# Two PSUM banks for exponentials taken one bank at a time, four for maxima taken two banks at a time, and the loops of layer 1 written out

## The chip, the cores and the metric

The kernel runs on one NeuronCore of a Trainium2 chip. The metric is the device time of one execution in microseconds (us). The kernel before was timed in three runs: median 14171.25 us, from 14164.81 to 14183.32.

The engines that matter are TensorE (PE in the profile, with its weight loads as PEld), VectorE (DVE), ScalarE (ACT) and, less, GpSimd (POOL) and the DMA queues of SyncE (SP) and POOL. Each works through its own list of instructions in order; semaphores tie them together.

## The reference

Two layers on an image batch x of 8 x 56 x 56 x 128. Layer 0 is a spectral mixing layer and is not touched by the change. Layer 1 is attention with 8 heads of 16 channels over the 3136 positions of each image, a residual and a layer norm:

```python
q = proj(wq, bq)
k = proj(wk, bk)
v = proj(wv, bv)
scores = jnp.einsum('bhqd,bhkd->bhqk', q, k) / jnp.sqrt(jnp.float32(d_k))
scores = scores + _spatial_bias_matrix(spatial_bias, H, W)[None, None]
attn = jax.nn.softmax(scores, axis=-1)
ctx = jnp.einsum('bhqk,bhkd->bhqd', attn, v)
...
resid = out + x_seq
...
out = (resid - mu) * jax.lax.rsqrt(var + LN_EPS) * ln_gamma + ln_beta
```

The bias of a score depends only on the distance of the two positions, rows plus columns, so it is added by a matmul over a small window table.

## The kernel before

Layer 0 takes the first 1.5 ms, some tables 0.3 ms more, and layer 1 the rest, from about 1.8 ms to the end.

**Tiling of layer 1.** Images `B` = 8, groups of four heads `NG` = 2, chunks `NC` = 7 of `CH` = 448 queries (8 rows of 56). So there are 112 chunks, numbered n. Within a chunk the 3136 keys are worked through in `EX` = 56 steps k: t = k // 2 is a tile of 112 keys and k % 2 a pair of the four heads. The softmax needs the largest score of each query first, so a chunk has two jobs that run side by side: the exponentials of chunk n, and the maxima of chunk n + 1 (`MX` = 112 tiles i of 112 queries x 448 keys).

**TensorE's order within a step k** is written out by hand (the function `step` at L1021 to L1053):

- `scores(g, k, between)` makes the scores of two heads e = 0, 1: two matmuls of keys by queries (L914, side by side in one PSUM bank) and two that add the bias (L918). Between e = 0 and e = 1 it calls `between`, that is `next_max`.
- `next_max` issues, if one is due, the two matmuls of one tile of maxima (`max_scores`, L947). `ahead(k, g, c)` says how many tiles are due by step k: all 112 in the first 49 steps, 16 in 7 steps, so that a step has 2 or 3 of them. An even step calls `next_max` before its scores (step 0 twice), then between the heads, after them, and last; an odd step has no call before its scores. In chunk 6 of a group the maxima begin at step 4 (`K_LATE`), in chunk 0 of an image at step 6 (`K_NEXT`).
- In odd steps from 3 on, `weigh` multiplies the exponentials of steps k - 3 and k - 2 with the values (L930, eight fp32 matmuls, in four column groups side by side). The last two steps of a chunk are weighed in step 0 of the next.
- Side work in the bank `MB`: the sums of the chunk before at step 3 (L982), its output product at step 10 for the second group (L989), the row maxima at step 52 (`turn_rows`, L956), and in chunk 5 of a group the projections of the next group, one of 42 pieces a step from step 12 (L967, L971, L975).

**ScalarE** takes one exponential a step (L1116) over two PSUM banks, 120 partitions x 896, into one of four buffers `p`; at step 2 it copies the context of the chunk before (L1094), at step 52 two row maxima (L1089), and in chunk 5 the projections (L1080). **VectorE** takes a maximum for every tile i (`find_max`, L1194), 120 x 448 each, and does the small work: copies for the next chunk (L1178, L1188, L1189), reciprocals at steps 5 to 8 (L1214), the layer norm of the second group from step 11, the split of the projections (L1161). **GpSimd** converts projections and issues loads and stores, **SyncE** issues the keys of the maxima (`key_win`).

**PSUM's eight banks** are shared out at L716: four for scores awaiting the exponential (`SB`), two for each step, so TensorE may fill step k while ScalarE reads step k - 1; one for the context (`CB`); two for the maxima (`AB`); one for side work (`MB`).

**The waits.** `exp_ready` is raised once a step, and `exp_done` once a step (it starts at 2). Before the scores of step k TensorE waits until the exponential of step k - 2 is done (L1034); before the maxima of tile i it waits until tile i - 2 has been reduced (L944).

**Loops.** `images` runs seven images in a hardware loop and writes the eighth out; `chunks` writes out chunks 0, 5 and 6 of a group and runs chunks 1 to 4 in a hardware loop, on TensorE, ScalarE and VectorE. In a loop a wait's threshold is worked out in a register. SyncE and GpSimd have loops of their own over chunks.

## Time and profile before

| | us |
|---|---|
| median of 3 runs | 14171.25 (14164.81 to 14183.32) |
| the profiled execution: its own time | 14178.28 |
| its span, first to last instruction | 14176.7 |
| mean granted TensorE clock | 0.949 of full |
| PE busy | 13118.8 (93%) |
| DVE busy | 10007.6 (71%) |
| ACT busy | 6425.9 (45%) |
| POOL busy | 891.7 (6%) |

The span is the time from the first to the last instruction on the core; 1.6 us of the profiled execution's time lie outside it. Busy is the time in which an engine had at least one instruction in work; matmuls overlap, so for PE it says little about how densely the starts follow each other. For that one reads the starts in the timeline.

### The profile page before, as it was taken

What the parts mean: (1) busy time and instruction counts of PE and PEld (TensorE: products, weight loads), DVE (VectorE), ACT (ScalarE), POOL (GpSimd) and SP (SyncE); (2) the same over time, 40 slices, a digit from 0 to 9 for tenths busy, and PEclk for the clock granted to TensorE, in tenths of its full rate; (3) what the DMA queues carried; (4) which work ended last, traced back from release to release, by engine and by line L of the source; (5) the groups of instructions that cost most, each with busy time, mean ns of one, the idle gap of its engine ahead of it and who ended that gap; (6) DMA issues with size and microseconds to landing.
All of it is one profiled execution on the core that took longest, in us unless ns stands there. A gap on an engine that the chain in (4) does not pass through costs nothing.

```text
span 14176.7 us, 304054 instructions
## 1 busy us (share of the span) xinstructions
PE 13118.8 (93%) x110635; PEld 5455.4 (38%) x110635; DVE 10007.6 (71%) x17426; ACT 6425.9 (45%) x7576; POOL 891.7 (6%) x1062
## 2 busy tenths in 40 slices
PE   8888479999999999999999999999999999999999
PEld 4444123333333333333333333333333333333333
DVE  3555167777777777777777777777777777777776
ACT  1111025554555545554555455545555455545555
POOL 0222110001000000000000100000000000010000
PEclk8888569999999999999999999999999999999999
DMA  3443122222222222222222222222222222222121
GB/s 65 88 88 80 43 41 35 39 41 40 36 37 42 40 38 37 41 40 39 36 40 38 42 35 37 42 40 39 38 39 40 39 40 37 39 42 40 36 38 30
DMA packets 317569, 607.72 MB, mean 43 GB/s; under 512 B 63894, under 2 KB 248750, under 8 KB 315054
## 3 DMA queue, kind: packets, MB, share of 16 engines
q1 hardware_dynamic: 294618, 535.94, 20.8%
q0 software_dynamic: 21504, 51.47, 1.3%
q8 instruction: 1033, 16.92, 0.5%
q14 instruction: 414, 3.39, 0.1%
HBM read 328.18 MB, written 53.47 MB: 27 GB/s over the span
## 4 chain that ended last, share of the span: by engine, by line
PE 71%; DVE 9%; issue 5%; ACT 2%; DVEq 0%; SPq 0%; DMA 0%; ACTq 0%; POOL 0%; POOLq 0%
PE l_ps L947 18%; PE l_ps L930 17%; PE l_ps L914 15%; PE l_ps L918 15%; DVE partial L1194 6%; PE l_ps L971 3%; PE l_ps L989 1%; PE l_ps L982 1%; ACT q_max L1089 1%; PE l_ps L975 1%; ACT p L1116 1%; DVE recip L1214 1%; DVE win_exp L1189 0%; DVE qs L1161 0%; DVE ks L1161 0%
## 5 line engine op out<-in xcount | busy, mean ns | idle before, releaser
L1194 DVE TENSOR_REDUCE partial<-l_ps 120x1 f32<-120x448 f32 x12544 | 7356.3, 621 | 2001.3 <-PE l_ps L947 1988.3
L1116 ACT ACTIVATE p<-l_ps 120x896 f32<-120x896 f32 x6272 | 5722.9, 917 | 5605.3 <-PE l_ps L918 5536.5
L947 PE MATMUL l_ps<-key_win,q_pick 128*56 128x448 f16 (+1 forms) x25088 | 4482.2, 365 | 407.4 <-DVE partial L1194 259.9
L914 PE MATMUL l_ps<-q_exp,ks 65*56 65x448 f16 (+1 forms) x25088 | 4543.4, 361 | 40.5 <-DVE win_exp L1189 27.7
L918 PE MATMUL l_ps<-win_exp,fold 112*56 112x448 f16 x25088 | 4513.8, 359 | 0.0
L930 PE MATMUL l_ps<-p,v 120*32 120x448 f32 x25088 | 3052.5, 559 | 2.1 <-ACT p L1116 2.1
L947 PEld LDWEIGHTS l_ps<-key_win,q_pick 128*64 128x64 f16 (+1 forms) x25088 | 1331.5, 108 | 3913.8 <-DVE partial L1194 3171.9
L914 PEld LDWEIGHTS l_ps<-q_exp,ks 65*64 65x64 f16 (+1 forms) x25088 | 1403.1, 110 | 1189.2 <-issue 282.6
L918 PEld LDWEIGHTS l_ps<-win_exp,fold 112*56 112x56 f16 x25088 | 1381.3, 109 | 924.3 <-issue 42.4
L930 PEld LDWEIGHTS l_ps<-p,v 120*32 120x32 f32 x25088 | 499.6, 109 | 1052.4 <-issue 1021.1
L866 POOL CAST half<-full 128x448 f16<-128x448 f32 x448 | 270.4, 604 | 5959.3 <-ACT full L1080 5959.3
L392 PE MATMUL l_ps<-G,Y 112*120 112x448 f32 x1024 | 425.7, 581 | 140.0 <-DVE Y L564 140.0
L1205 DVE CAST q_max<-l_ps 1x448 f16<-1x448 f32 x224 | 138.3, 617 | 521.8 <-PE l_ps L956 518.4
L881 POOL DMA_DIRECT2D out<-res x112 | 72.1, 648 | 5635.0 <-DVE res L1295 5069.4
L1214 DVE RECIPROCAL recip<-l_ps 128x112 f32<-128x112 f32 x448 | 376.2, 845 | 69.7 <-PE l_ps L982 69.7
L573 DVE TENSOR_TENSOR x<-l_ps,x 56x448 f32<-56x448 f32 x256 | 159.0, 621 | 289.5 <-PE l_ps L392 285.5
L1161 DVE SCALAR_TENSOR_TENSOR qs<-half,flags_sb,full 64x448 f16<-64x448 f16 x448 | 304.1, 679 | 66.1 <-POOL half L866 34.7
L392 PEld LDWEIGHTS l_ps<-G,Y 112*120 112x120 f32 x1024 | 201.7, 199 | 360.7 <-issue 328.7
L1161 DVE SCALAR_TENSOR_TENSOR ks<-half,flags_sb,full 64x448 f16<-64x448 f16 x448 | 306.1, 683 | 25.7 <-ACT q_max L1089 8.9
L479 ACT COPY xt<-l_ps 128x448 f32<-128x448 f32 x32 | 17.0, 532 | 584.4 <-PE l_ps L416 584.4
L971 PE MATMUL l_ps<-xT,wk 128*128 128x448 f32 x448 | 243.5, 627 | 38.3 <-DVEq L1207 27.6
L1080 ACT ACTIVATE full<-l_ps,bq 128x448 f32<-128x448 f32 x224 | 142.3, 635 | 285.3 <-PE l_ps L971 274.1
(135 smaller groups left out, 5520.5 us busy)
## 6 DMA issues: line engine op xcount, KB each, us to landing
key_win<-ks SPq DMA_DIRECT2D x1792, 112.0 KB, 2.8
key_win<-by_query_scratch SPq DMA_DIRECT2D x224, 868.0 KB, 5.9
x<-in_x SPq DMA_DIRECT2D x16, 1568.0 KB
xc<-y_scratch POOLq DMA_DIRECT2D x224, 112.0 KB, 2.7
h_scratch<-x SPq DMA_DIRECT2D x8, 1568.0 KB
w_scratch<-x SPq DMA_DIRECT2D x8, 1568.0 KB
mh<-h_scratch SPq DMA_DIRECT2D x64, 196.0 KB
mw<-w_scratch SPq DMA_DIRECT2D x64, 196.0 KB
```

Of the source, the lines that this page charges most:

```text
L392: last = nc.tensor.matmul(ps[0:GP + W, IB + i % 2, 0:HALF], w["Y"][:, k, (i // 2) * 2 * GP:(i // 2) * 2 * GP + GP + W], w["G"][r][:, k, (i ...
L573: nc.vector.tensor_tensor(dst, ps[GP * odd:GP * odd + W, IB + i % 2, 0:HALF].rearrange("p (t s) -> p t s", s=S), dst, ALU.add).then_inc(ad ...
L866: nc.gpsimd.tensor_copy(half[m][:], full[m][:]).then_inc(proj_half, 1)
L914: nc.tensor.matmul(ps[r * GP:r * GP + m, bank, 0:CH], ks[g][:, j, k0:k0 + m], q_exp[:, j, :], start=True, stop=True)
L918: last = nc.tensor.matmul(ps[r * GP:r * GP + W, bank, 0:CH], fold16[:], win_exp[:, s0:s0 + CH], start=False, stop=True, skip_group_check=True)
L930: last = nc.tensor.matmul(ps[32 * j:32 * j + 32, CB, 0:CH], v[g][:, v0:v0 + 32], p[k % 4][:, e, :], start=t == 0, stop=t == NT - 1, skip_g ...
L947: last = nc.tensor.matmul(ps[r * GP:r * GP + wide, AB + i % 2, 0:CH], q_pick[:, j, q0:q0 + wide], rows(key_win[place][:])[:, s0:s0 + QC, 0 ...
L971: nc.tensor.matmul(ps[:, MB, 0:CH], (wk4 if i % 2 == 0 else wq4)[:, h:h + 2, :].rearrange("c h k -> c (h k)"), rows(xT[:])[:, :, 0:W], sta ...
L1116: nc.scalar.activation(p[k % 4][:], ps[0:GP + W, bank:bank + 2, 0:CH], ACT.Exp).then_inc(exp_done, 1)
L1161: last = nc.vector.scalar_tensor_tensor(dst, rows(half[pn % 3][part, :], W), w["flags"][part, 0:1] if is_k else w["flags"][part, 1:2], row ...
L1194: nc.vector.tensor_reduce(partial[:, tile, kc:kc + 1], ps[0:GP + W, AB + i % 2, 0:CH], AX.X, ALU.max).then_inc(max_done, 1)
L1214: nc.vector.reciprocal(recip[:, cut], ps[:, MB, cut]).then_inc(recip_done, 1)
```

## The change

PSUM is shared out anew: two banks for scores awaiting the exponential (`SB` = 0), four for maxima (`AB` = 2), then the context (`CB` = 6) and side work (`MB` = 7). Each head e of a step has one bank. TensorE raises `exp_ready` after each head, ScalarE takes the exponential of one bank (120 x 448) and raises `exp_done` after each, and before the scores of head e in step k TensorE waits for the exponential of the same head in step k - 1. The maxima are reduced in pairs of tiles: one VectorE instruction over two banks (120 x 2 x 448) for each odd i, and TensorE waits before every even i from 4 on until the pair before the last has been reduced. The loops over images and over chunks 1 to 4 are written out for every engine that uses these two helpers: TensorE, ScalarE and VectorE wholly; GpSimd's images too, while its inner loops and SyncE's remain.

```diff
--- before.py
+++ after.py
@@ -713,7 +713,7 @@
         res_in, res = sb("res_in", [KT, UT, C]), sb("res", [KT, UT, C])
         stat = sb("stat", [KT, 3, UT])
         ps = ctx.enter_context(nc.psum_tensor("l1_ps", [128, 8, 512], F32))
-        SB, CB, AB, MB = 0, 4, 5, 7
+        SB, AB, CB, MB = 0, 2, 6, 7
 
         loaded, set_up, clear = sem("l1_loaded"), sem("l1_set_up"), sem("clear")
         xc_in, xt_ready = [sem(f"xc{i}_in") for i in range(2)], sem("l1_xt_ready")
@@ -784,15 +784,14 @@
             return FIRST + b * SIDES + place[g, 1, what] + (c - 1) * (place[g, 2, what] - place[g, 1, what])
 
         def images(eng, image):
-            with eng.Fori(0, B - 1) as b:
-                image(b, False)
-            image(B - 1, True)
+            for b in range(B):
+                image(b, b == B - 1)
 
         def chunks(eng, g, last, step):
 
             final = last and g == NG - 1
             step(0, None if g == 0 else NC - 1, True, False)
-            with eng.Fori(1, C_PREP) as c:
+            for c in range(1, C_PREP):
                 step(c, c - 1, True, False)
             step(C_PREP, C_PREP - 1, True, not final)
             step(NC - 1, NC - 2, not final, False)
@@ -904,11 +903,12 @@
 
         @block.tensor
         def _(pe):
-            def scores(g, k, between):
+            def scores(g, n, k, between):
 
                 t, pair = k // 2, k % 2
                 for e in range(2):
-                    j, bank = 2 * pair + e, SB + 2 * pair + e
+                    j, bank = 2 * pair + e, SB + e
+                    pe.wait_ge(exp_done, 2 * (n * EX + k) + e + 1)
                     for r, m in enumerate((GP, W)):
                         k0 = (2 * t + r) * RP
                         nc.tensor.matmul(ps[r * GP:r * GP + m, bank, 0:CH], ks[g][:, j, k0:k0 + m], q_exp[:, j, :],
@@ -917,9 +917,9 @@
                         s0 = (H - 1 - 2 * t - r) * W
                         last = nc.tensor.matmul(ps[r * GP:r * GP + W, bank, 0:CH], fold16[:], win_exp[:, s0:s0 + CH],
                                                 start=False, stop=True, skip_group_check=True)
+                    last.then_inc(exp_ready, 1)
                     if e == 0:
                         between()
-                last.then_inc(exp_ready, 1)
 
             def weigh(g, k):
 
@@ -939,12 +939,12 @@
                     pe.wait_ge(win_in[place], (m + 1) * 16)
                 if kc == 0:
                     pe.wait_ge(keys_in[place], (m * UT * HG // 2 + tile // 2 + 1) * 16)
-                if i >= 2:
-                    pe.wait_ge(max_done, m * MX + i - 1)
+                if i >= 4 and i % 2 == 0:
+                    pe.wait_ge(max_done, m * (MX // 2) + i // 2 - 1)
                 s0 = QC * kc - 2 * u + QC - 2
                 for r, wide in enumerate((GP, W)):
                     q0 = u * KT + r * W
-                    last = nc.tensor.matmul(ps[r * GP:r * GP + wide, AB + i % 2, 0:CH], q_pick[:, j, q0:q0 + wide],
+                    last = nc.tensor.matmul(ps[r * GP:r * GP + wide, AB + i % 4, 0:CH], q_pick[:, j, q0:q0 + wide],
                                             rows(key_win[place][:])[:, s0:s0 + QC, 0:W], start=True, stop=True)
                 last.then_inc(score_ready, 1)
 
@@ -1026,14 +1026,13 @@
                             if k == 0:
                                 next_max()
                                 if before is not None:
-                                    pe.wait_ge(exp_done, 2 + n * EX)
+                                    pe.wait_ge(exp_done, 2 + 2 * n * EX)
                                     for i in (EX - 2, EX - 1):
                                         weigh(g if not (isinstance(c, int) and c == 0) else 1 - g, i)
 
-                            pe.wait_ge(exp_done, 2 + n * EX + k - 1)
                             if k == 0:
                                 pe.wait_ge(staged_exp, HEAD + (n + 1) * 2)
-                            scores(g, k, next_max)
+                            scores(g, n, k, next_max)
                             next_max()
 
                             if k > 1 and k % 2:
@@ -1056,7 +1055,7 @@
                     chunks(pe, g, last, step)
                 n = b * NG * NC + NG * NC - 1
                 for k in range(2):
-                    pe.wait_ge(exp_done, 2 + n * EX + EX - 1 + k)
+                    pe.wait_ge(exp_done, 2 + 2 * (n * EX + EX - 1 + k))
                     weigh(1, EX - 2 + k)
                 spread_sums(n, side(b, last, "end", 0, "sum"))
                 mix(n, side(b, last, "end", 0, "mix"))
@@ -1111,9 +1110,9 @@
                             if k == K_CTX and before is not None:
                                 copy_context(n - 1)
                             act.wait_ge(pv_done, 4 + n * EX + k - 3)
-                            act.wait_ge(exp_ready, HEAD + n * EX + k + 1)
-                            bank = SB + 2 * (k % 2)
-                            nc.scalar.activation(p[k % 4][:], ps[0:GP + W, bank:bank + 2, 0:CH], ACT.Exp).then_inc(exp_done, 1)
+                            for e in range(2):
+                                act.wait_ge(exp_ready, HEAD + 2 * (n * EX + k) + e + 1)
+                                nc.scalar.activation(p[k % 4][:, e, :], ps[0:GP + W, SB + e, 0:CH], ACT.Exp).then_inc(exp_done, 1)
                             if maxima and k == K_ROWS:
                                 copy_rows(side(b, last, g, c, "rows"))
                             if projections and K_PREP <= k < K_PREP + PREP:
@@ -1183,19 +1182,21 @@
                 nc.vector.tensor_copy(q_pick[0:DK], qs[0:DK, :, bass.ds(c * CH, CH)]).then_inc(staged_pick, 1)
 
             def stage_exp(n, c):
-                dve.wait_ge(exp_ready, HEAD + n * EX)
+                dve.wait_ge(exp_ready, HEAD + 2 * n * EX)
                 dve.wait_ge(row_copied, (n + 1) * HG)
                 nc.vector.tensor_copy(q_exp[:], q_max[:]).then_inc(staged_exp, 1)
                 nc.vector.tensor_copy(win_exp[:], w["by_key"][:, bass.ds(c * QC * W, STG_K)]).then_inc(staged_exp, 1)
 
             def find_max(i, base):
-                tile, kc = i // NC, i % NC
+                if i % 2 == 0:
+                    return
+                bank = AB + i % 4 - 1
                 dve.wait_ge(score_ready, AHEAD + base + i + 1)
-                nc.vector.tensor_reduce(partial[:, tile, kc:kc + 1], ps[0:GP + W, AB + i % 2, 0:CH], AX.X,
-                                        ALU.max).then_inc(max_done, 1)
+                nc.vector.tensor_reduce(partial[:].rearrange("p t k -> p (t k)")[:, i - 1:i + 1], ps[0:GP + W, bank:bank + 2, 0:CH],
+                                        AX.X, ALU.max).then_inc(max_done, 1)
 
             def join_max(m):
-                dve.wait_ge(max_done, (m + 1) * MX)
+                dve.wait_ge(max_done, (m + 1) * (MX // 2))
                 nc.vector.tensor_reduce(neg_max[:], partial[:], AX.X, ALU.max, negate=True).then_inc(neg_ready, 1)
 
             def copy_rows(m, n):
@@ -1364,7 +1365,7 @@
                             stage_pick(m + 1, b * 0)
                         elif isinstance(c, int) and c == NC - 1 and maxima:
                             stage_pick(m + 1, b * 0 + 1)
-                        elif not isinstance(c, int) or c == 0:
+                        elif c < C_PREP:
                             stage_pick(m + 1, c + 2)
                     chunks(dve, g, last, step)
                 n = b * NG * NC + NG * NC - 1
```

## Rows read from the trace of the kernel before

**Rows 1.** The page: busy time by engine, one queue's instruction fetches, the chain by engine

```profile
PE 13118.8 (93%) x110635; PEld 5455.4 (38%) x110635; DVE 10007.6 (71%) x17426; ACT 6425.9 (45%) x7576; POOL 891.7 (6%) x1062
...
q8 instruction: 1033, 16.92, 0.5%
...
PE 71%; DVE 9%; issue 5%; ACT 2%; DVEq 0%; SPq 0%; DMA 0%; ACTq 0%; POOL 0%; POOLq 0%
```

**Rows 2.** Windows of image 2's chunks 1, 2, 5: length, busy PE, PEld, DVE, ACT, POOL, clock

```profile
3625.80:3723.90 98.10, 96.14 (x918) 38.36 (x914) 73.31 (x126) 52.56 (x60) 0.00 (x0) 1.00 0.22 39
3723.90:3826.70 102.80, 99.17 (x918) 39.26 (x914) 73.45 (x126) 52.61 (x60) 0.00 (x0) 0.97 0.21 37
...
4029.70:4178.70 149.00, 141.73 (x1056) 56.64 (x1058) 112.64 (x188) 73.75 (x94) 24.71 (x40) 0.96 0.15 28
```

**Rows 3.** Timeline of TensorE in steady steps: start, us, instruction, [idle before <-releaser]

```profile
3741.46 0.35 PE L918 MATMUL l_ps<-win_exp,fold 112*56 112x448 f16 x2
...
3742.23 0.35 PE L914 MATMUL l_ps<-q_exp,ks 65*64 65x448 f16 x2
...
3743.47 0.96 PE L930 MATMUL l_ps<-p,v 120*32 120x448 f32 x8
3744.36 0.57 PE L947 MATMUL l_ps<-key_win,q_pick 128*64 128x448 f16 x4
...
3744.96 0.35 PE L918 MATMUL l_ps<-win_exp,fold 112*56 112x448 f16 x2
3745.47 0.38 PE L947 MATMUL l_ps<-key_win,q_pick 128*64 128x448 f16 x2 [0.15 <-DVE partial L1194]
```

**Rows 4.** Timeline of ScalarE: the exponential after the L918 at 3742.04

```profile
3742.44 1.88 ACT L1116 ACTIVATE p<-l_ps 120x896 f32<-120x896 f32 x2 [1.43 <-PE l_ps L918]
```

**Rows 5.** Timeline in chunk 5 of the last image, where no loop encloses the step

```profile
13988.85 0.35 PE L918 MATMUL l_ps<-win_exp,fold 112*56 112x448 f16 x2
...
13989.31 0.92 ACT L1116 ACTIVATE p<-l_ps 120x896 f32<-120x896 f32 x1 [1.96 <-PE l_ps L918]
```

**Rows 6.** Timeline of steps 53 to 55: exponentials behind the row copies, scores that waited

```profile
3824.07 2.88 ACT L1116 ACTIVATE p<-l_ps 120x896 f32<-120x896 f32 x3
...
3825.04 0.38 PE L914 MATMUL l_ps<-q_exp,ks 65*64 65x448 f16 x2
```

**Rows 7.** Groups by line and shape, ScalarE: busy us, mean ns of one

```profile
L1116 ACT ACTIVATE p<-l_ps 120x896 f32<-120x896 f32 x6272 | 5722.9, 917 | 5605.3 <-PE l_ps L918 5536.5 <-ACT xT L1071 0.2
L1080 ACT ACTIVATE full<-l_ps,bq 128x448 f32<-128x448 f32 x224 | 142.3, 635 | 285.3 <-PE l_ps L971 274.1 <-DVE ks L1161 11.2
...
L470 ACT ACTIVATE mean_t<-l_ps 128x56 f32<-128x56 f32 x16 | 2.6, 205 | 17.4 <-PE l_ps L402 17.4
```

**Rows 8.** The same view, VectorE's reductions

```profile
L1194 DVE TENSOR_REDUCE partial<-l_ps 120x1 f32<-120x448 f32 x12544 | 7356.3, 621 | 2001.3 <-PE l_ps L947 1988.3
...
L1261 DVE TENSOR_REDUCE stat<-res_in 112x4 f32<-112x512 f32 x56 | 38.0, 679 | 0.5
```

**Rows 9.** Timeline from chunk 0 to 1 (no branch), then from 2 to 3 (branch)

```profile
3624.72 0.35 PE L918 MATMUL l_ps<-win_exp,fold 112*56 112x448 f16 x2
...
3627.28 0.38 PE L914 MATMUL l_ps<-q_exp,ks 65*64 65x448 f16 x2
...
3628.32 0.38 PE L947 MATMUL l_ps<-key_win,q_pick 128*64 128x448 f16 x2 [0.48 <-DVE partial L1194]
...
3825.64 0.35 PE L918 MATMUL l_ps<-win_exp,fold 112*56 112x448 f16 x2
...
3829.21 0.95 PE L947 MATMUL l_ps<-key_win,q_pick 128*64 128x448 f16 x4 [2.33 <-issue]
...
3831.74 0.58 PE L914 MATMUL l_ps<-q_exp,ks 65*64 65x448 f16 x2
```

**Rows 10.** Timeline of TensorE in chunk 5 with projections

```profile
4088.15 0.38 PE L947 MATMUL l_ps<-key_win,q_pick 128*64 128x448 f16 x2 [1.38 <-DVE partial L1194]
...
4091.15 1.02 PE L971 MATMUL l_ps<-xT,wq 128*128 128x448 f32 x2
```

## The prediction

> **What bounds the kernel now.** I read the page first: TensorE is busy 93%, VectorE 71%, ScalarE 45%, and the chain that ended last lies to 71% on TensorE and to 9% on VectorE [rows 1]. So TensorE sets the time and the other two cost something only where it waits. How much it waits is in the starts of its matmuls, not in its busy time. Next come windows over single chunks of layer 1: chunk 1 of image 2 takes 98.10 us, chunk 2, which ends in a branch, 102.80, and chunk 5, with projections, 149.00 [rows 2]. In the timeline two steps in a steady stretch are a dense row of slots: from the bias matmuls of the first head to the next step's first scores it is four slots in 0.77, so 0.193 a slot [rows 3]. A chunk has 336 such slots (64.8 us), 28 weighings of 0.89 (3743.47 to 3744.36 [rows 3]) with some 0.09 ahead of each, an estimate (27.4), and the sums (about 1.0, one matmul like that of [rows 10]): 93.2 us with no wait at all. The 98.10 of chunk 1 hold 4.9 us of waits, chunk 2 a further 4.7.
>
> **Edit 1, exponentials of one bank (loses).** Before, the scores of step k needed the exponential of step k - 2. Now head e needs that of head e in step k - 1. Odd steps end with a weighing (0.98 us), which covers this. The crossing from an even to an odd step has no such cover. Its price has four parts.
>
> (a) Matmul to exponential. In a loop the bias matmul at 3742.04 (a slot before the scores at 3742.23 [rows 3]) is followed by its exponential at 3742.44 [rows 4]: 0.40. In the written-out chunk 5 of the last image it is 13988.85 to 13989.31, 0.46 [rows 5]. 
> (b) The exponential of 448. The trace has none. 896 elements take 917 ns and 56 take 205 ns [rows 7], so 0.848 ns an element and 448 take 0.54. Bounds: 0.46, half of 917, and 0.635, an activation of 448 with a bias column [rows 7]. I take 0.54, since line and operands stay the same.
> (c) Back to TensorE. The exponentials from 3824.07 are three; the first ends at 3824.99 and the scores behind it start at 3825.04: 0.05. A matmul that restarts so takes 0.38 in place of 0.35 [rows 3, 6], and the next starts about 0.02 late.
> (d) The distance that is there. With one tile of maxima in between (kind A) 0.77, with a second behind head 1 (B) 0.96, with none (C) 0.58.
>
> The need is 0.46 + 0.54 + 0.05 = 1.05. So A waits 0.28, B 0.09, C 0.47, with the restart 0.30, 0.11, 0.49; for C head 1 is late by 0.03 too, 0.52. Head 1 is else in time: its exponential is due back 1.57 after head 0's bias matmul and its slot comes at 1.65.
> The counts follow from `ahead`: a chunk 1 to 4 has 19 A (steps 0, 2, 4, ... with two tiles), 6 or 7 B (three tiles, and step 52, where the row maxima stand between) and 2 C (50, 54). Chunk 5 has 5 A and 1 C, since side matmuls of up to 1 us fill every step from 12; chunk 6 has 1 A, 23 B, 4 C; the last chunk of all, without maxima, 27 C. Over 112 chunks: 1549 A, 936 B, 288 C. Sum: 465 + 103 + 150 = 718 us. Two places are worse, since ScalarE has something else in front: step 2 (the context copy) by about 0.15, and steps 53 to 55, where the exponentials start only behind the row copies [rows 6] and the scores now need them a step earlier, by about 0.25, half an exponential. That is 0.4 x 112 = 45. In all 763.
> By the Trainium skill (ScalarE: Activation LUTs, its part on what an ACTIVATE costs) one with immediate operands takes 186 ns and 0.833 ns an element, 0.56 for 448. Here 896 elements measured 917 ns where that rule gives 932, so I keep 0.54; by the rule the sum would be 55 us higher.
> What stands behind the new wait on TensorE is everything, since it works in order: the maxima, head 1, the weighing; so VectorE gets its tiles later by as much, and needs them less. The key loads on SyncE's queue wait for maxima long made, as before. The second count of `exp_ready` rides on a matmul that is there.
>
> **Edit 2, maxima by two banks (gains).** The reduction of 448 takes 621 ns and one of 512 takes 679, 0.91 ns an element [rows 8]; two banks take about 1.05 to 1.09 against 2 x 0.58 in a full queue. That saving is off the path. What counts is the slack: TensorE may be two to three tiles further ahead. Now a third tile waits when two follow each other: at 3744.36 two in a row, and the next comes at 3745.47, 0.51 after the bias matmul in place of 0.19 [rows 3]. With the restart that is 0.34, about 6.5 times a chunk: 2.2. At the chunk's start one waits 0.48 [rows 9], at the reciprocals about 0.8 more. Together 3.5 us of the 4.9. The new distance from the second tile of a pair to the first of the pair after next is at least three tile distances, 0.19 + 0.58 + 0.96 = 1.73, and the need 0.40 + 1.09 + 0.05 = 1.54: no wait, unless VectorE has another operation in between. 73 regular chunks (1 to 4, chunk 0 of group 1, the last 5) x 3.5 = 255. Chunk 5: work without waits is 93.2 and the side matmuls, 28 of about 0.96 [rows 10] and 7 x 1.3 for the short ones, 129 in all, against 98 + 36 = 134 at the regular chunk's waits and 149.00 measured; one wait is 1.38 for VectorE [rows 10]. Of these 15 to 20 us VectorE explains a part; I take 6.5, bounds 0 and 13. 15 x 6.5 = 98. Chunk 6 and chunk 0 of group 0 together about 45. Sum 398; bounds 200 (pairs hold up VectorE's other work) and 670 (every wait in the chunks: 4.9 x 97 + 13 x 15).
> In straight code a matmul with two waits (keys and `max_done`) starts 0.04 later; nine of them a chunk, partly given back: 17 us lost.
>
> **Edit 3, loops written out (gains).** From the last bias matmul of chunk 0 to the first scores of chunk 1, with no branch taken, it is 3624.72 to 3627.28, 2.56; with the branch, from chunk 2 to 3, 3825.64 to 3831.74, 6.10, with 2.33 of issue, and the matmuls come at half clock behind it (0.58 for 0.38) [rows 9]. So 3.5 us a branch, 3 branches in each of 16 groups: 167 us. The seven image branches stand behind waits for the layer norm's inputs and give perhaps 3 in all. Register arithmetic in the loops costs nothing now: the 98.10 chunk is in a loop and has it. Fetching: the queue moved 1033 pieces, 16.92 MB [rows 1], which is already the whole executed program, so straight code fetches no more. The prologue's 112 maxima gain about 12.
>
> **Sum.** 763 + 17 - 398 - 167 - 3 - 12 = +200 us on the profiled execution's 14178.28, so 14378. That execution stands 7 us above the median of the runs; against those, 14371.
>
> **Rivals.**
> Forecast: the crossings cost more than slack and branches give, 14371, its own range 14270 to 14480. Chance 0.55.
> No change: head 0's exponential keeps its 0.40. Then each of the 2773 crossings costs 0.06 less, 166 us, and the time is 14205, around the upper edge of no change. Against it speaks every step of the written-out chunks [rows 5]. Chance 0.12.
> Faster: TensorE's waits for the maxima go wholly, 670 in place of 398, also in chunk 5: 200 - 272 = -72, 14099. It decides from 598 us on. For it speaks that VectorE gets 7% of its work back and TensorE twice the slack; against it that chunk 5's waits also come from chains of projections over three engines. Chance 0.14.
> Slower still: VectorE waits for both tiles of a pair with splits and reciprocals queued behind, who free the bank for side work; the gain halves to 200 and chunk 5 grows by 2: 14371 + 198 + 30 = 14600. Chance 0.13.
> The branches' gain doesn't come, since the stall was fetching and straight code stalls as well: 14540. Against it: chunks 4 to 5 to 6 are straight already and go on without a gap. Chance 0.06.
>
> **How the numbers follow.** About 0.2% (28 us) is what a measurement can tell: below 14143 is faster, to 14199 the same. Faster 0.14 and a little of the no-change case, 0.16; same 0.09; slower 0.75. The range runs from 14085 (the faster case in) to 14560; outside are the slower case's 0.13 and the tails of the others.
>
> **What would show it.** L1116 has twice the count at 0.53 to 0.55 each, 0.46 behind the matmul for head 0; idle of L914 before ScalarE's release rises from almost nothing to some 600 us; L1194 halves its count at about 1.09; TensorE's idle before L947 shrinks; no 2.33 of issue between chunks. A regular chunk 1 takes about 102.5 us (98.1 - 3.5 + 7.9). I am wrong if the exponential's start is 0.40 for both heads, if a chunk 5 falls by over 10 us, or if the crossings are hidden by waits that I take to be gone.

## The result, and the profile after

| | before | changed |
|---|---|---|
| median of 6 runs, us | 14170.3 (14164.81 to 14191.61) | 14237.95 (14237.24 to 14240.86) |
| ratio to before, 95% interval | | 1.0045 (1.0032 to 1.0058) |
| span of the profiled execution | 14176.7 | 14239.3 |
| mean granted clock | 0.949 | 0.959 |

The change makes the kernel slower by 0.45%, and the interval lies clear of 1: 68 us by the medians, 63 by the spans of the two profiled executions, which the sums below use. The forecast was 200 us slower. The sign and the mechanism hold, the size is a third of it.

The page of the changed kernel, in order the lines that answer to [rows 1] and two groups that answer to [rows 7, 8]:

```profile
PE 13293.4 (93%) x110635; PEld 5200.0 (37%) x110635; DVE 9484.1 (67%) x11154; ACT 7252.3 (51%) x13848; POOL 889.2 (6%) x1062
...
q8 instruction: 847, 13.88, 0.4%
...
PE 74%; ACT 9%; DVE 2%; issue 2%; ACTq 0%; SPq 0%; DMA 0%; DVEq 0%; POOL 0%; POOLq 0%
...
L1115 ACT ACTIVATE p<-l_ps 120x448 f32<-120x448 f32 x12544 | 6553.4, 543 | 4783.4 <-PE l_ps L918 4704.8
L1195 DVE TENSOR_REDUCE partial<-l_ps 120x2 f32<-120x896 f32 x6272 | 6785.9, 1088 | 2544.9 <-PE l_ps L947 2477.2
```

VectorE lost 523 us of work and ScalarE gained 826, and on the chain that ended last they changed places: it lay to 9% on VectorE and to 2% on ScalarE, and is now 2% and 9%. The exponential of 448 takes 543 ns and the reduction over two banks 1088 ns.

Where TensorE itself stood idle is in the groups of its matmuls (busy us, mean ns, idle before them and its releasers). Before, scores and maxima:

```profile
L914 PE MATMUL l_ps<-q_exp,ks 65*56 65x448 f16 (+1 forms) x25088 | 4543.4, 361 | 40.5 <-DVE win_exp L1189 27.7 <-issue 3.0 <-ACT p L1116 2.8
L947 PE MATMUL l_ps<-key_win,q_pick 128*56 128x448 f16 (+1 forms) x25088 | 4482.2, 365 | 407.4 <-DVE partial L1194 259.9 <-issue 113.5 <-DMA key_win<-ks 6.8
```

The same two groups of the changed kernel:

```profile
L914 PE MATMUL l_ps<-q_exp,ks 65*56 65x448 f16 (+1 forms) x25088 | 4564.2, 363 | 302.8 <-ACT p L1115 113.5 <-DVE win_exp L1188 7.6
L947 PE MATMUL l_ps<-key_win,q_pick 128*64 128x448 f16 (+1 forms) x25088 | 4399.9, 361 | 34.8 <-DVE partial L1195 21.1 <-DMA key_win<-ks 7.0
```

The 113.5 us of issue (the branches) are gone, of the 260 us behind VectorE 21 are left, and 303 us stand before the scores instead of 40. These sums show the direction only: a matmul's modelled end hides most of a short wait, so sizes come from starts, below.

The windows of [rows 2], image 2, chunks 1, 2 and 5 (length, then busy time of PE, PEld, DVE, ACT and POOL, clock, DMA share, GB/s), now:

```profile
3622.30:3724.80 102.50, 99.42 (x918) 36.08 (x914) 68.23 (x69) 60.24 (x115) 0.00 (x0) 1.00 0.20 36
3724.80:3827.30 102.50, 99.41 (x918) 36.09 (x914) 68.23 (x69) 60.15 (x115) 0.00 (x0) 1.00 0.21 37
...
4032.40:4176.30 143.90, 140.72 (x1058) 55.76 (x1058) 108.32 (x132) 79.99 (x150) 24.59 (x40) 0.97 0.16 29
```

Chunk 1 went from 98.10 to the forecast 102.5, chunk 2 lost its branch and is now equal to it, chunk 5 gained 5.1.

The forecast crossing of kind A, in the timeline (start, duration; some rows left out):

```profile
3741.17 0.35 PE L918 MATMUL l_ps<-win_exp,fold 112*56 112x448 f16 x2
...
3741.63 1.06 ACT L1115 ACTIVATE p<-l_ps 120x448 f32<-120x448 f32 x2 [1.48 <-PE l_ps L918]
...
3742.22 0.38 PE L914 MATMUL l_ps<-q_exp,ks 65*64 65x448 f16 x2
```

Bias matmul at 3741.17, its exponential 0.46 later, 0.54 in work, and the next step's scores at 3742.22: 1.05, the need worked out in the prediction. There is no weighing in between, so all of it shows. Over the chunks 1 to 4 of all images the median is 0.459 for head 0 and 0.399 for head 1; for the single exponential of a step it was 0.399 in the loops of the kernel before. From chunk 1 to chunk 2, where nothing branches now:

```profile
3723.32 0.35 PE L918 MATMUL l_ps<-win_exp,fold 112*56 112x448 f16 x2
...
3725.88 0.38 PE L914 MATMUL l_ps<-q_exp,ks 65*64 65x448 f16 x2
```

That is 2.56, as at the boundary without a branch of [rows 9], against 6.10 with one.

### The profile page after: what moved, and what is told of

It is laid out like the page before. It is cut to its first block, busy times and chain, and to the rows that moved or that the text cites. A ratio compares the mean times of both kernels' runs of the same rounds, so it can differ in the third digit from the quotient of the medians.

```text
span 14239.3 us, 268044 instructions
## 1 busy us (share of the span) xinstructions
PE 13293.4 (93%) x110635; PEld 5200.0 (37%) x110635; DVE 9484.1 (67%) x11154; ACT 7252.3 (51%) x13848; POOL 889.2 (6%) x1062
## 3 DMA queue, kind: packets, MB, share of 16 engines
q8 instruction: 847, 13.88, 0.4%
## 4 chain that ended last, share of the span: by engine, by line
PE 74%; ACT 9%; DVE 2%; issue 2%; ACTq 0%; SPq 0%; DMA 0%; DVEq 0%; POOL 0%; POOLq 0%
PE l_ps L930 19%; PE l_ps L914 18%; PE l_ps L947 17%; PE l_ps L918 14%; ACT p L1115 8%; PE l_ps L971 3%; PE l_ps L989 1%; PE l_ps L975 1%; PE l_ps L982 1%; DVE partial L1195 1%; ACT q_max L1088 1%; DVE qs L1160 0%; PE l_ps L967 0%; ACTq L1114 0%; ACT full L1079 0%
## 5 line engine op out<-in xcount | busy, mean ns | idle before, releaser
L1115 ACT ACTIVATE p<-l_ps 120x448 f32<-120x448 f32 x12544 | 6553.4, 543 | 4783.4 <-PE l_ps L918 4704.8
L1195 DVE TENSOR_REDUCE partial<-l_ps 120x2 f32<-120x896 f32 x6272 | 6785.9, 1088 | 2544.9 <-PE l_ps L947 2477.2
L914 PE MATMUL l_ps<-q_exp,ks 65*56 65x448 f16 (+1 forms) x25088 | 4564.2, 363 | 302.8 <-ACT p L1115 113.5
L918 PE MATMUL l_ps<-win_exp,fold 112*56 112x448 f16 x25088 | 4467.9, 356 | 0.0
L947 PE MATMUL l_ps<-key_win,q_pick 128*64 128x448 f16 (+1 forms) x25088 | 4399.9, 361 | 34.8 <-DVE partial L1195 21.1
L914 PEld LDWEIGHTS l_ps<-q_exp,ks 65*56 65x56 f16 (+1 forms) x25088 | 1361.7, 107 | 2904.6 <-ACT p L1115 2443.2
L947 PEld LDWEIGHTS l_ps<-key_win,q_pick 128*56 128x56 f16 (+1 forms) x25088 | 1331.7, 109 | 2852.6 <-issue 1902.8
L918 PEld LDWEIGHTS l_ps<-win_exp,fold 112*56 112x56 f16 x25088 | 1360.5, 108 | 479.7 <-issue 6.4
```

What stands on the lines that cost most here:

```text
L914: nc.tensor.matmul(ps[r * GP:r * GP + m, bank, 0:CH], ks[g][:, j, k0:k0 + m], q_exp[:, j, :], start=True, stop=True)
L918: last = nc.tensor.matmul(ps[r * GP:r * GP + W, bank, 0:CH], fold16[:], win_exp[:, s0:s0 + CH], start=False, stop=True, skip_group_check=True)
L947: last = nc.tensor.matmul(ps[r * GP:r * GP + wide, AB + i % 4, 0:CH], q_pick[:, j, q0:q0 + wide], rows(key_win[place][:])[:, s0:s0 + QC, 0 ...
L1115: nc.scalar.activation(p[k % 4][:, e, :], ps[0:GP + W, SB + e, 0:CH], ACT.Exp).then_inc(exp_done, 1)
L1195: nc.vector.tensor_reduce(partial[:].rearrange("p t k -> p (t k)")[:, i - 1:i + 1], ps[0:GP + W, bank:bank + 2, 0:CH], AX.X, ALU.max).then ...
```

## The experiments

Where a chunk's or a pair of steps' time is given, it is the spacing of the starts of their first score matmuls in the timeline, as a mean over the images. "Group 0" and "group 1" are the head groups. A pair of steps is an even step and the odd one behind it. The experiments fall in three sets, each with its own runs of the kernel before, to which its ratios refer: medians 14186.88, 14189.81 and 14181.06 against the 14170.3 above. A difference of 10 or 20 us between times of different sets is therefore not read from them alone.

### The three parts taken apart

**Loops alone**: the kernel before, with both helpers written out.

```diff
-            with eng.Fori(0, B - 1) as b:
-                image(b, False)
-            image(B - 1, True)
+            for b in range(B):
+                image(b, b == B - 1)
...
-            with eng.Fori(1, C_PREP) as c:
+            for c in range(1, C_PREP):
```

> The kernel before with its loops over images and chunks 1 to 4 written out, banks as before. By the terms of the prediction: 170 us less for the branches, 17 us more for matmuls with two waits, so 14017. Revised theory, after the result: the changed kernel is 137 us below the sum, of which 59 lie in chunk 0 of an image (105.47 us before, 103.58 after, where the sum had +5.5); there VectorE idled 2.33 us for issue between the end of the layer norm and its next copy (3533.43 to 3535.77), which is the image branch on VectorE, so the loops bring 30 to 60 more: 13960 to 13990. Rival: that surplus comes from the four banks for the maxima, not from the loops: 14017 or a little above, and chunk 0 of an image stays near 103 to 105.

Measured: 13976.86 us, ratio 0.9857 (0.984 to 0.9873). The loops' end is worth 197 us by the spans (14176.7 to 13979.9), 210 by the medians of its set. The time lies in the range of the revised theory, but not for its reason: chunk 0 of an image only went from 105.47 to 104.47 us, and 163 of the 197 us are in the chunks 1 to 4 and chunk 0 of group 1.

**Loops and exponentials**: the changed kernel with the maxima as they were, two banks and one tile to an instruction.

```diff
-                if i >= 4 and i % 2 == 0:
-                    pe.wait_ge(max_done, m * (MX // 2) + i // 2 - 1)
+                if i >= 2:
+                    pe.wait_ge(max_done, m * MX + i - 1)
...
-ps[r * GP:r * GP + wide, AB + i % 4, 0:CH]
+ps[r * GP:r * GP + wide, AB + i % 2, 0:CH]
```

> The changed kernel, but with the maxima as before: two banks, one tile to a reduction. Theory additive: loops_only plus the 763 us of the crossings. With 13975 for loops_only that is 14738. Theory overlapping (mine now): a wait for VectorE ahead of the tile between the heads also gives ScalarE time, so about a quarter of the crossings cost nothing: 14520 to 14600. The distance from the changed kernel, 14238, is what the four banks bring: 500 or 280 to 360.

Measured: 14614.11 us, ratio 1.0308 (1.0291 to 1.0325), span 14611.2. So on top of the loops the exponentials cost 631 us (forecast 763), and from here to the changed kernel the maxima's four banks give 372 (forecast 410 with the prologue). Plain addition fails, and of the two theories the overlapping one is nearer, though about a sixth of the crossings' price was covered and not a quarter.

**Image loop alone** written out, chunks 1 to 4 still in their loop.

```diff
-            with eng.Fori(0, B - 1) as b:
-                image(b, False)
-            image(B - 1, True)
+            for b in range(B):
+                image(b, b == B - 1)
```

> The kernel before with only the loop over images written out; chunks 1 to 4 stay in loops. Revised theory (the image branch delays VectorE, and through it the maxima): 30 to 60 us less than before, 14110 to 14140, with no idle for issue ahead of the q_max copy in chunk 0 of an image. By the prediction (image branches worth about 3 us): 14167. Since chunks 1 to 4 keep their branches, their mean stays at 100.6 us in group 0.

Measured: 14167.17 us, ratio 0.9988 (0.9978 to 0.9997), a gain between 4 and 31 us. The number is the prediction's 14167 by chance, since this set's kernel before stands at 14186.88. The theory that an image's first chunk is long because VectorE takes its branch late falls: that chunk still takes 104.1 us in group 0 (105.5 before).

### Chunk 0 of an image: a wait that was there already

With loops gone, chunk 0 of group 0 takes 104.47 us against 98.16 for its neighbours. The timeline of the loops-alone kernel in image 3, steps 5 to 7:

```profile
6511.93 0.35 PE L946 MATMUL l_ps<-key_win,q_pick 128*56 128x448 f16 x2
...
6513.27 0.69 DVE L1294 TENSOR_TENSOR res<-res_in,beta 112x512 f32<-112x512 f32 x1
6513.88 0.61 DVE L1177 COPY q_max<-qs 64x1792 f16<-64x1792 f16 x1
6514.42 1.71 DVE L1193 TENSOR_REDUCE partial<-l_ps 120x1 f32<-120x448 f32 x3
6515.08 0.38 PE L946 MATMUL l_ps<-key_win,q_pick 128*64 128x448 f16 x2 [2.42 <-DVE partial L1193]
...
6515.82 0.58 PE L946 MATMUL l_ps<-key_win,q_pick 128*56 128x448 f16 x2
```

VectorE finishes the layer norm of the image before (L1294) and a copy ahead of its first maxima; TensorE's third tile waits 2.42 us, and its matmuls are at half clock behind that (0.58 for 0.35; the granted clock is 0.50 from 6515.5 to 6518.9, and it was full during the wait and for the 7 us before). In the changed kernel the same place in image 3:

```profile
6606.12 0.69 DVE L1296 TENSOR_TENSOR res<-res_in,beta 112x512 f32<-112x512 f32 x1
...
6607.27 2.07 DVE L1195 TENSOR_REDUCE partial<-l_ps 120x2 f32<-120x896 f32 x2
...
6608.40 0.38 PE L947 MATMUL l_ps<-key_win,q_pick 128*64 128x448 f16 x2 [0.61 <-DVE partial L1195]
```

TensorE comes here later, since its steps 0 to 5 waited for exponentials (10.3 us for these six steps in place of 8.1, means over the images), and has four tiles' room; 0.61 is left. Two kernels leave the long part of that norm out, in the kernel with loops alone and in the changed one:

```diff
+                if brief:
+                    dve.sem_inc(norm_step, LINKS)
+                    dve.wait_ge(norm_step, (n + 1) * LINKS)
+                    nc.vector.tensor_tensor(res[:], res_in[:], each(beta), ALU.add).then_inc(out_ready, 1)
+                    yield
+                    return
                 link(nc.vector.tensor_tensor(res[:], res[:], each(bo), ALU.add))
```

> loops_only with the layer norm of each image's last chunk cut down to its first and last operation (that chunk's output is not normalised), so that VectorE is free when the next image begins. Theory: in loops_only TensorE waits about 5 us at steps 6 and 7 of chunk 0 of an image for VectorE (9.4 to 9.6 us for these two steps in place of 3.7), so chunk 0 falls from 104.5 to 98.5 to 99.5 us. Rival: these steps wait for a load of keys or for the clock, and stay above 8 us.

> The changed kernel with the same cut to the last layer norm of each image (that chunk's output is not normalised). It tells whether the crossings in chunk 0 of an image cost what the sum charged (6.8 to 7.4 us) or were covered by the wait for VectorE at step 6. With the norm: 104.47 us in loops_only, 103.58 in the changed kernel, 0.9 less. Theory (covered): without it loops_only is at 99.74 and the changed kernel falls only by 1 or so, to 102.5 to 103, so that it is 3 us slower there. Rival (four banks gain that much there by themselves): it falls by as much as loops_only did, to about 99.

Measured, one execution each: 13943.94 us (33 less than with the norm) and 14215.55 us (22 less). Chunk 0 falls from 104.47 to 99.74 with loops alone, a little above the 98.5 to 99.5 expected, and its steps 6 and 7 take 3.69 us in every image, in place of 7.9 to 9.6 behind a layer norm. So it is VectorE's layer norm that they waited for, and not the keys. In the changed kernel the chunk falls from 103.58 to 102.46. So the change costs this chunk 2.7 us without the norm and -0.9 with it: here 3.6 us of new crossings were covered by a wait for VectorE.

### Are pairs what gains, or four banks?

**Four banks, single tiles**: the changed kernel, each tile reduced by itself.

```diff
-                if i >= 4 and i % 2 == 0:
-                    pe.wait_ge(max_done, m * (MX // 2) + i // 2 - 1)
+                if i >= 4:
+                    pe.wait_ge(max_done, m * MX + i - 3)
...
-                nc.vector.tensor_reduce(partial[:].rearrange("p t k -> p (t k)")[:, i - 1:i + 1], ps[0:GP + W, bank:bank + 2, 0:CH],
-                                        AX.X, ALU.max).then_inc(max_done, 1)
+                nc.vector.tensor_reduce(partial[:, tile, kc:kc + 1], ps[0:GP + W, AB + i % 4, 0:CH], AX.X,
+                                        ALU.max).then_inc(max_done, 1)
```

> The changed kernel with four banks for the maxima, but one reduction to each tile as before. If the slack of the banks is what removes TensorE's waits: 14228 to 14250, the same as the changed kernel, with VectorE busier by some 500 us. If the 12% less of VectorE's work matter, above all in chunk 5 where it also splits projections: 14270 to 14330.

Measured: 14214.4 us, ratio 1.0021 (1.0011 to 1.0031), 24 us faster than pairs by the medians and 34 by the spans, and so faster than either expectation. Its page:

```profile
PE 13240.9 (93%) x110635; PEld 5208.9 (37%) x110635; DVE 10009.3 (70%) x17426; ACT 7247.7 (51%) x13848; POOL 899.2 (6%) x1062
...
L1193 DVE TENSOR_REDUCE partial<-l_ps 120x1 f32<-120x448 f32 x12544 | 7338.9, 620 | 1947.1 <-PE l_ps L947 1901.4
```

VectorE does 525 us more (5% of its work, not 12%) and the kernel is not slower: the whole gain is in the depth, 400 us from two banks (14614) to four. Regular chunks are the same (102.40 against 102.52 in group 0); of the 34 us of the spans 32 are in the chunks with projections (141.29 against 143.74, and 143.58 against 145.39). That a pair frees its banks only when both tiles are read would explain this; it was not shown by itself.

### The crossing: its first term and its distance

**Waits swapped**: before the exponential, ScalarE waits for the scores of head 0 first and for `pv_done` second.

```diff
-                            act.wait_ge(pv_done, 4 + n * EX + k - 3)
                             for e in range(2):
                                 act.wait_ge(exp_ready, HEAD + 2 * (n * EX + k) + e + 1)
+                                if e == 0:
+                                    act.wait_ge(pv_done, 4 + n * EX + k - 3)
```

> The changed kernel with the two waits of head 0's exponential written in the other order (exp_ready, then pv_done), nothing else. Theory: which wait becomes an instruction of its own follows the order in the code, so head 0's exponential then starts 0.40 instead of 0.46 us behind its matmul, and each of the 2773 crossings costs 0.06 less: 166 us, 14072; less where the crossing is covered, so 14070 to 14110. Rival: the order doesn't matter or the start doesn't set the crossing: 14238.

Measured: 14093.86 us, ratio 0.9934 (0.9917 to 0.9951), 144 below the changed kernel (the prediction had 166 for it). A crossing of kind A in its timeline:

```profile
3740.52 0.35 PE L918 MATMUL l_ps<-win_exp,fold 112*56 112x448 f16 x2
...
3740.92 2.33 ACT L1116 ACTIVATE p<-l_ps 120x448 f32<-120x448 f32 x4 [1.23 <-PE l_ps L918]
...
3741.52 0.38 PE L914 MATMUL l_ps<-q_exp,ks 65*64 65x448 f16 x2
```

Head 0's exponential comes 0.40 behind its bias matmul in place of 0.46, the next scores after 1.00 in place of 1.05. Pairs of steps of kind A take 3.56 in place of 3.62, of kind C 3.03 in place of 3.09. The trace records it: in the changed kernel an EVENT_SEMAPHORE of 0.017 us waits for the scores (3741.565, line 1114) and head 0's ACTIVATE starts 0.062 later; with the waits swapped the ACTIVATE carries that wait itself and the instruction on its own is the one for `pv_done` (3741.503, line 1115). So of two waits the one written first rides on the ACTIVATE and the second becomes an instruction of its own, and it is worth 0.06 us where that second one is the critical one.

**Tile moved**: in even steps the tile of maxima ahead of head 0's scores goes behind head 1's, which widens the distance at the crossing.

```diff
-                            if k % 2 == 0:
-                                next_max()
                             if k == 0:
                                 next_max()
+                                next_max()
```

> The changed kernel with the tile of maxima that an even step issues ahead of its scores moved behind head 1 (step 0 keeps its two). Every crossing with two tiles (1549 of kind A, 0.77 us of distance) becomes one of kind B (0.96). Theory: each costs 0.11 instead of 0.30, 294 us less: 13944. Rival: VectorE's waits come back, since two tiles then follow more closely around the crossing: 14100 or more.

Measured: 14088.59 us, ratio 0.993 (0.9913 to 0.9946): 149 us gained, half of what was expected. Kind A is gone, but its place was not free. Its timeline in a step with three tiles:

```profile
3750.23 2.09 DVE L1194 TENSOR_REDUCE partial<-l_ps 120x2 f32<-120x896 f32 x2 [1.07 <-PE l_ps L947]
...
3750.41 0.54 PE L947 MATMUL l_ps<-key_win,q_pick 128*64 128x448 f16 x4
3750.79 0.35 PE L914 MATMUL l_ps<-q_exp,ks 65*64 65x448 f16 x2
3750.98 0.35 PE L918 MATMUL l_ps<-win_exp,fold 112*56 112x448 f16 x2
3751.38 0.38 PE L947 MATMUL l_ps<-key_win,q_pick 128*64 128x448 f16 x2
```

Two tiles come together at 3750.41, the one after them at 3751.38, 0.40 behind the bias matmul in place of 0.19: a wait for a pair. And chunk 6 of group 0 grew from 100.98 to 104.06 us, where nearly every pair of steps now takes 3.72 us in place of 3.62. That three tiles in a row against pairs is where the other half went is what the next kernel tries.

**Tile moved, single tiles**: the same on top of four single banks.

```diff
-                            if k % 2 == 0:
-                                next_max()
                             if k == 0:
                                 next_max()
+                                next_max()
```

> Four banks with one reduction to each tile, and the tile moved behind head 1; the waits of head 0 in the order of the changed kernel. tile_moved gained only 149 us of 294. Theory: there two tiles follow each other behind head 1 and the next pair waits for VectorE's two-bank reduction; with single reductions each bank comes free by itself, so this runs 294 us below four_single's 14214: 13920, 170 below tile_moved. Rival: the moved tile gains as little here, since it is the crossing that stays long: 14050 or more.

Measured: 13853.61 us, ratio 0.9767 (0.975 to 0.9783). The move gives 361 us here (14214 to 13854), against 149 under pairs: the pairs did hold it back. It is 67 more than the theory has, because it also helps in places where the theory has nothing: chunk 6 falls by 2.4 us and chunk 0 of group 0 by 2.2, 54 us in all.

**Both moves, single tiles**: waits swapped as well.

```diff
-                            act.wait_ge(pv_done, 4 + n * EX + k - 3)
                             for e in range(2):
                                 act.wait_ge(exp_ready, HEAD + 2 * (n * EX + k) + e + 1)
+                                if e == 0:
+                                    act.wait_ge(pv_done, 4 + n * EX + k - 3)
```

> Waits in the other order, the tile moved behind head 1, and one reduction to each tile in four banks (the variant that was 24 us faster than pairs). Theory: crossings with a tile behind head 1 need 0.99 and have 0.96, 0.05 with the restart; those without one still miss 0.41. 14214 - 387 - 56 - 17 = 13754, below the kernel before (14171) and below loops written out alone (13977). Rival: something else sets the pace once the crossings are short, VectorE or the array: 13900 to 13977.

Measured: 13744.02 us, ratio 0.9689 (0.9672 to 0.9705), faster than both kernels and than loops alone. The page and the two TensorE groups of this kernel:

```profile
PE 12972.1 (94%) x110635; PEld 5204.5 (38%) x110635; DVE 9917.3 (72%) x17426; ACT 7373.4 (54%) x13848; POOL 901.3 (7%) x1062
...
PE 78%; ACT 4%; DVE 4%; issue 1%; SPq 0%; DMA 0%; ACTq 0%; DVEq 0%; POOL 0%; POOLq 0%
```

```profile
L914 PE MATMUL l_ps<-q_exp,ks 65*64 65x448 f16 (+1 forms) x25088 | 4588.1, 365 | 122.6 <-ACT p L1115 90.6 <-DVE win_exp L1188 15.7
L947 PE MATMUL l_ps<-key_win,q_pick 128*56 128x448 f16 (+1 forms) x25088 | 4298.8, 356 | 16.3 <-DMA key_win<-ks 7.8 <-DVE partial L1193 7.7
```

The time is 10 us below the expected 13754; the swap alone gives 110 us here. Chunks 1 to 4 of group 0 take 97.24 us each, against 102.52 in the changed kernel and 98.16 with loops alone: the banks are those of the changed kernel, with one tile at another place, each reduced alone, and two waits in the other order. No run tries the moved tile with the old banks, so how much of the 233 us that this kernel is faster than loops alone needs the new ones isn't shown.

### The new banks with the chunk loops kept

```diff
-            for c in range(1, C_PREP):
+            with eng.Fori(1, C_PREP) as c:
```

> The changed kernel with chunks 1 to 4 back in hardware loops (images stay written out). 165 us more for the 48 branches; but in a loop register arithmetic takes the first wait, so head 0's exponential starts 0.40 behind its matmul there and 28 crossings in each of 64 chunks cost 0.06 less, 107 us: 14238 + 165 - 107 = 14296. Rival: the start doesn't depend on the loop, 14403.

Measured: 14398.63 us, ratio 1.0151 (1.0134 to 1.0168), 103 above the expectation. The time is almost the 14403 of the rival, but by coincidence: the 0.40 for both heads in loops came as expected (median 0.399 each, kind A 3.56). The branch did not; from chunk 2 to 3 it is

```profile
3838.77 0.35 PE L918 MATMUL l_ps<-win_exp,fold 112*56 112x448 f16 x2
...
3843.03 0.68 PE L947 MATMUL l_ps<-key_win,q_pick 128*64 128x448 f16 x4 [3.02 <-issue]
3845.29 0.58 PE L914 MATMUL l_ps<-q_exp,ks 65*64 65x448 f16 x2
```

3.02 us of issue and 6.52 from bias matmul to scores, where [rows 9] had 2.33 and 6.10, and a half-clock stretch behind it: from its first scores on, layer 1 spent 492 us at the lower clock, 241 in the changed kernel. Chunks 1 to 4 hold three branches; they take 104.87 us each in group 0 and 107.43 in group 1, against 100.97 and 102.96 with none and the waits swapped, so a branch costs this kernel 5.2 to 6.0 us. In the kernel before it is 3.2 to 3.7 (100.56 and 103.44 against 98.16 and 100.69 with loops alone). Why a branch costs the new banks more is open. The stretches at the lower clock don't explain it: from the first scores on they are 506 us before and 270 with loops alone, a difference as large. And with the waits in the changed kernel's order, writing out the chunk loops is worth 161 us (14398.63 to 14237.95), less than the 190 that it gives the old banks (14167.17 to 13976.86), since it also brings 0.06 to each crossing; only with the waits swapped is it worth more to the new banks (305 us, some of it the swap in the other chunks).

## Why the prediction came out three times too high

By the spans the forecast was -153 for the loops (branches -167, images -3, two-wait matmuls +17), +763 for the exponentials, -410 for the maxima with the prologue: +200. Measured: -197, +631, -372: +63. Every part had its sign, and the prices of one crossing, one branch and one reduction held. What failed is how they were multiplied. The errors are 132 us (exponentials) and 44 (loops) one way and 38 (maxima) the other, so that they offset each other a little.

**Right.** Step (a), 0.46 for head 0; (b), 0.54 measured as 543 ns; (c) and (d), so kind A 3.62 us a pair of steps where 3.61 follows, C 3.09 where 3.06 does. By the Trainium skill (ScalarE: Activation LUTs, "What ACT_TABLE_LOAD costs", which also prices an ACTIVATE) the exponential would be 559 ns, an estimate from its rule; the trace says 543. The reduction of two banks, 1.05 to 1.09, measured 1.088. The branch, 3.5 us: 2.56 in place of 6.10 at one boundary, 3.2 to 3.7 by chunks. A regular chunk, 102.5. Chunk 5 gaining less than 10: 3.3 and 7.3. The idle before L914 rose, but the page's rows can't give the "some 600": the group shows 303.

Net of the loops (changed against loops alone) by kind of chunk, what the prediction's counts and prices give and what was measured:

| | chunks | forecast each | measured each | difference in all |
|---|---|---|---|---|
| regular (1 to 4; chunk 0 of group 1) | 72 | +4.35 | +4.15 | -14 |
| with projections (chunk 5) | 15 | -4.1 | -4.4 | -5 |
| chunk 6 | 15 | +3.3 | +1.65 | -25 |
| chunk 0 of group 0 | 8 | +5.3 | -0.9 | -50 |

**The step that failed: the counts of crossings.** All 2773 were priced in full, also where TensorE waited at the same place for something else, and where the time lost in a crossing only shortened a later wait.
- Chunk 0 of group 0: the waits of its first steps shorten the wait for the layer norm at step 6, as the short-norm kernels show (3.6 us of the 6.2 that are missing; the rest is open). The prediction knew the layer norm only as a cover for the image branch.
- Chunk 6: in group 0 its steps 2 and 3 took 6.13 us before and 5.25 with loops alone, with no maxima issued and the context copy in front of the exponentials; now 4.30, where the sum had a crossing and 0.15 more. Why they were so long before isn't shown.
- Even in a regular chunk the two halves of the sum are not independent. With the old maxima the crossings cost 6.9 us, not the 7.85 forecast, since a crossing takes the place of a wait for a bank of the maxima; and so four banks then give 2.7, not 3.5. The starts of group 0 show it, from loops alone to loops and exponentials: a pair of steps without a wait for VectorE goes from 3.31 to 3.62 us, the full price; those of steps 14, 38 and 42, with such a wait, from 3.54 to 3.62; those of steps 8 and 10, behind the reciprocals, from 4.02 to 4.02 and 3.84 to 3.85; steps 0 and 1 stay at 3.09. The two errors cancel in the net, and only there: that is why 4.35 came out well and both 763 and 410 too high.

Of the 132 us that the crossings cost less than forecast, 70 are in the regular chunks, 35 in chunk 6 and 26 in chunk 0 of group 0. The maxima's term misses 55 in the regular chunks and gives 23 more than forecast in chunk 0 of group 0.

**The loops term, 44 us too small.** In the chunks 1 to 4 and chunk 0 of group 1 the loops' end gives 163 us, with the two-wait matmuls' loss in it, where 167 less their share of 17 is 156. Another 31 come from chunk 0 of group 0, chunk 5 and chunk 6 (8, 11 and 12), where the sum had images -3 and the rest of +17, so nothing. Some 17 of them may be the image loop's (interval 4 to 31). The remainder I can't place.

**The rivals.** "No change, head 0 keeps its 0.40" was wrong as an account of this kernel, since the trace has 0.46; but its price of 0.06 a crossing is right, and with the waits swapped it is there to be had. "TensorE's waits for the maxima go wholly": on the page they nearly do (21 of 260 us left), but what that gave was 372 us and not 670, and regular chunks gave less than the forecast's 3.5. The 7% of VectorE's work that was to speak for it measured 523 of 10007.6 us, 5%. "VectorE waits for both tiles of a pair": joining them costs the chunk with projections 2 us and the kernel 24 to 34, not the 200 of that rival. "The branches' gain doesn't come": it came, and straight code did not fetch as much as before, as the prediction had it, but less (13.88 MB in place of 16.92).

## What to carry to other kernels

A wait that a change adds is worth its price only where nothing else holds the engine in the same few microseconds, so count places by what waits there now, chunk kind by chunk kind, not by the instruction's occurrences. Fewer banks for one producer cost latency at each handover: look for the place where the order gives that handover the least distance and put other work there, before the banks are shared out anew; here one moved tile, two swapped waits and single reductions turn a loss of 0.45% into a gain of 3.1%, of which the loops alone are 1.4%. Two operations in one instruction save the engine time but hand back their buffers together; where the depth is what gains, keep them single.

## What the runs showed of the hardware that was not expected

- On ScalarE, in written-out code, the order of two waits ahead of one instruction decides whether it starts 0.40 or 0.46 us behind the last matmul that releases it: the wait that is written second stands as an instruction of its own in the trace. Over the changed kernel that is 144 us.
- A taken branch of TensorE's long loop is not one price: 2.33 us of issue in the kernel before and 3.02 with the new banks, with 3.2 to 3.7 and 5.2 to 6.0 us in all, with a stretch at the lower clock behind it. By the Trainium skill (Runtime: NRT & Kernel Launch, "Instruction fetch mechanics") a branch to code outside what is fetched stalls until it is read in. The traces agree as far as they go: no issue time stands at the chunk boundaries without a branch, and the queue that fetches moved 1033 pieces before, 847 in the changed kernel. Writing the loops out did not make the fetching dearer, it made it less. Why the price differs between the two kernels is not shown.
- Behind the wait of 2.42 us at step 6 TensorE's matmuls took 0.58, at a granted clock of 0.50; behind the 0.61 in the same place of the changed kernel the clock stayed full: they started 0.19 apart and took 0.35. Part of what a wait costs or saves can be the clock behind it.
